# P V of the second and third attention: two column tiles a head, or one full matmul

## What is computed

```python
x = x + jnp.tanh(g_xattn[1]) * attn1(_layernorm(x), ctx)      # plain softmax
x = x + jnp.tanh(g_ffn[1])   * quantised_mlp(_layernorm(x))
x = x + jnp.tanh(g_xattn[2]) * attn2(_layernorm(x), ctx, mask)  # masked softmax
x = x + jnp.tanh(g_ffn[2])   * top2_experts(_layernorm(x))

qh, kh, vh = split_heads(q), split_heads(k), split_heads(v)   # 16 heads of 8
score = einsum('bhqd,bhkd->bhqk', qh, kh) / sqrt(8)
out = einsum('bhqk,bhkd->bhqd', softmax(score), vh)           # this is P V
```

## Time and profile before

| what | value |
| --- | --- |
| median of 3 runs | 2514.34 us (2514.01 to 2516.51) |
| the profiled execution's own time | 2513.01 us |
| its span, first to last instruction | 2511.2 us |
| mean granted TensorE clock | 0.915 |
| second attention, steady step (L1012 to L1012) | 7.44 us |
| third attention, two late steps (1598.4 to 1619.5) | 21.1 us |

### The profile page before, as it was taken

One profiled execution on the slowest core, in us unless ns is written; L12 is line 12 of the kernel. 1 busy time (PEld: TensorE's weight loads), 2 busy tenths in 40 slices (PEclk: granted clock), 3 DMA queues, 4 the chain that ended last, 5 costly groups with the idle time before them and its releaser, 6 DMA issues. The chain is left out here.

```text
span 2511.2 us, 81208 instructions
## 1 busy us (share of the span) xinstructions
PE 2146.8 (85%) x33432; PEld 1717.8 (68%) x33443; DVE 1787.9 (71%) x5105; ACT 1350.6 (54%) x2499; POOL 1157.7 (46%) x1712
## 2 busy tenths in 40 slices
PE   6999999999995969999555799998399958898597
PEld 5887878787874746777444577776399947777375
DVE  3777777777773648887896589886555559988354
ACT  3555555555551327886998455553122259979232
POOL 1333333434343541113776125555466666876444
PEclk8999999999997979998677899997699979989699
DMA  6330000000005621110000111111487622332363
GB/s 194 110 123 27 25 27 25 24 21 20 20 18 152 180 85 55 55 58 17 1 1 3 32 37 52 52 51 36 134 235 230 185 75 79 106 96 79 101 185 103
DMA packets 225233, 195.14 MB, mean 78 GB/s; under 512 B 34444, under 2 KB 197846, under 8 KB 224864
## 3 DMA queue, kind: packets, MB, share of 16 engines
q1 hardware_dynamic: 186336, 143.52, 19.6%
q0 software_dynamic: 18944, 36.98, 4.2%
q10 hardware_dynamic: 19584, 9.44, 1.3%
HBM read 113.53 MB, written 70.55 MB: 73 GB/s over the span
## 5 line engine op out<-in xcount | busy, mean ns | idle before, releaser
L617 POOL DMA_INDIRECT slots<-row,put x256 | 258.1, 1008 | 211.5 <-issue 131.2
L1968 PE MATMUL experts_H<-experts_xs_t,experts_w 128*128 128x256 f32 (+1 forms) x832 | 253.5, 456 | 9.9 <-DMA experts_w<-in_F_w 4.7
L1102 ACT ACTIVATE l_prob_t<-l_banks 128x512 f32<-128x512 f32 x256 | 132.2, 603 | 145.9 <-PE l_banks L1219 115.4
L1968 PEld LDWEIGHTS experts_H<-experts_xs_t,experts_w 128*128 128x128 f32 x832 | 156.7, 195 | 74.5 <-issue 54.0
L1474 POOL TENSOR_TENSOR l_var_eps<-l_mv,eps 128x1 f32<-128x1 f32 x64 | 12.1, 189 | 413.9 <-DVE l_mv L1555 413.9
L1277 PE MATMUL l_banks<-l_val,l_prob_t 128*64 128x18 f32 x5120 | 201.1, 215 | 0.0
L1277 PEld LDWEIGHTS l_banks<-l_val,l_prob_t 128*64 128x64 f32 x5120 | 190.3, 143 | 8.1 <-issue 0.7
L1510 DVE TENSOR_REDUCE l_top<-l_S 128x16 f32<-128x1024 f32 x64 | 78.3, 1224 | 161.7 <-PE l_S L1653 161.7
L1986 PE MATMUL experts_Y<-experts_w,experts_hid 128*128 128x128 f32 x1600 | 190.0, 275 | 3.5 <-DVE experts_y L1912 2.6
L1986 PEld LDWEIGHTS experts_Y<-experts_w,experts_hid 128*128 128x128 f32 x1600 | 184.3, 192 | 5.0 <-issue 4.9
L1823 POOL DMA_INDIRECT rows<-experts_y,experts_idx x144 | 139.9, 971 | 90.0 <-DVE experts_y L1908 52.9
(11 more groups left out here) (312 smaller groups left out, 5943.4 us busy)
## 6 DMA issues: line engine op xcount, KB each, us to landing
experts_w<-in_F_w SPq DMA_DIRECT2D x136, 256.0 KB
l_ctx_t<-in_ctx_t SPq DMA_DIRECT2D x96, 128.0 KB, 2.4
early_q_m<-l_q_t SPq DMA_DIRECT2D x384, 32.0 KB, 1.8
experts_xs<-slots SPq DMA_DIRECT2D x72, 132.0 KB
experts_w<-in_F_w ACTq DMA_DIRECT2D x72, 128.0 KB, 3.3
slots<-l_empty SPq DMA_DIRECT2D x16, 536.0 KB, 4.1
experts_xs<-slots SPq DMA_DIRECT2D x16, 536.0 KB
slots<-l_empty SPq DMA_DIRECT2D x16, 520.0 KB, 5.9
```

The lines of the kernel that those rows point to most:

```text
L617: pool.indirect_dma_start(self.slots, bass.IndirectOffsetOnAxis(ap=g.put[c][:, tile:tile + 1], axis=0), g.row[:, tile, self.sent_cols], No ...
L1102: nc.scalar.activation(prob_t[:, t.par(PROB), r, :], Z[:, r, :], ACT.Exp).then_inc(prob_done, 1)
L1968: last = nc.tensor.matmul(H[:, c, cols], w1_s[:, t.par(2, WS), h, c, :], xs_t[:, t.par(2), cols], start=True, stop=True)
```

## The change

In the second and third attention, one matmul a head takes both tiles: 128 stationary columns (64 queries of each tile) and 36 moving ones (18 of each tile). Of the 128 x 36 result only tile 0's rows with the first 18 columns and tile 1's rows with the last 18 are read. For the 128 columns to lie side by side, the exp writes `prob_t` with the tile inside the head: 128 j + 64 tile + query. The results need 16 x 64 columns and go to Z banks 2 and 3, so P V waits for the exp of bank 3. The reciprocal takes all four sums of a head and partition, 64 a partition instead of 32, and the product is made in two instructions, one for each half of the partitions. The fourth attention ("stable") keeps its form.

```diff
-        recip, ctx_out = ph.sb("recip", [P, 2, 16]), ph.sb("ctx_out", [P, 2, 2, D])
+        recip, ctx_out = ph.sb("recip", [P, 2, 16 if stable else 32]), ph.sb("ctx_out", [P, 2, 2, D])
@@ VectorE, OUT
-                    V.reciprocal(recip[:, :, :], o[:, :, :, 8]).then_inc(recip_done, 1)
+                    pairs = Z[:, 2:4, :].rearrange("p k (h c) -> p (k h) c", c=64)
+                    sums = o[:, :, :, 8] if stable else pairs[:, :, 8:36:9]
+                    V.reciprocal(recip[:, :, :] if stable else recip[:, :, :].rearrange("p k (h s) -> p (k h) s", s=4), sums).then_inc(recip_done, 1)
                     wait(dve, recip_done, t.done(OUT))
-                    V.tensor_tensor(ctx_out[:, t.par(OUT), :, :].rearrange("p b (h c) -> p b h c", c=8), o[:, :, :, 0:8],
+                    if not stable:
+                        for tile in range(2):
+                            rows = slice(64 * tile, 64 * tile + 64)
+                            pair = pairs[rows, :, 18 * tile:18 * tile + 18].rearrange("p h (b c) -> p b h c", c=9)
+                            by = recip[rows, :, :].rearrange("p k (h s) -> p s (k h)", s=4)[:, 2 * tile:2 * tile + 2, :]
+                            last = V.tensor_tensor(ctx_out[rows, t.par(OUT), :, :].rearrange("p b (h c) -> p b h c", c=8),
+                                                   pair[:, :, :, 0:8], by.unsqueeze(3).broadcast_to([64, 2, 16, 8]), ALU.mult)
+                        last.then_inc(o_drained, 1)
@@ ScalarE, PROB
-                            nc.scalar.activation(prob_t[:, t.par(PROB), r, :], Z[:, r, :], ACT.Exp).then_inc(prob_done, 1)
+                            nc.scalar.activation(prob_t[:, t.par(PROB), r, :].rearrange("p (j t n) -> p t j n", t=2, n=64),
+                                                 Z[:, r, :].rearrange("p (t j n) -> p t j n", t=2, n=64), ACT.Exp).then_inc(prob_done, 1)
@@ TensorE, OUT
-                        bank_read(t, 2)
-                    for h in range(16):
-                        terms = [prob_t] if not stable else [soft] if h // 4 < JOINED else [soft, prob_t]
+                        bank_read(t, 3)
+                    for h in range(16 if not stable else 0):
+                        pair = prob_t[:, t.par(OUT), h // 4, P * (h % 4):P * (h % 4) + P]
+                        last = nc.tensor.matmul(Z[:, 2 + h // 8, 64 * (h % 8):64 * (h % 8) + 36], pair,
+                                                val[:, t.par(OUT), :, h, :, :].rearrange("p t b c -> p t (b c)"), start=True, stop=True)
+                    for h in range(16 if stable else 0):
```

More of the change, by code:

```diff
@@ L1038, in step @@
                     wait(dve, o_filled, t.done(OUT))
-                    V.reciprocal(recip[:, :, :], o[:, :, :, 8]).then_inc(recip_done, 1)
+                    pairs = Z[:, 2:4, :].rearrange("p k (h c) -> p (k h) c", c=64)
+                    sums = o[:, :, :, 8] if stable else pairs[:, :, 8:36:9]
+                    V.reciprocal(recip[:, :, :] if stable else recip[:, :, :].rearrange("p k (h s) -> p (k h) s", s=4), sums).then_inc(recip_done, 1)
                     wait(dve, recip_done, t.done(OUT))
-                    V.tensor_tensor(ctx_out[:, t.par(OUT), :, :].rearrange("p b (h c) -> p b h c", c=8), o[:, :, :, 0:8],
+                    if not stable:
[6 more added lines that the diff above has]
+                        last.then_inc(o_drained, 1)
+                    else:
+                        V.tensor_tensor(ctx_out[:, t.par(OUT), :, :].rearrange("p b (h c) -> p b h c", c=8), o[:, :, :, 0:8],
                                     recip[:, :, :].unsqueeze(3).broadcast_to([P, 2, 16, 8]), ALU.mult).then_inc(o_drained, 1)
@@ L1270, in step @@
                     else:
-                        bank_read(t, 2)
-                    for h in range(16):
-                        terms = [prob_t] if not stable else [soft] if h // 4 < JOINED else [soft, prob_t]
+                        bank_read(t, 3)
[4 more added lines that the diff above has]
+                    for h in range(16 if stable else 0):
+                        terms = [soft] if h // 4 < JOINED else [soft, prob_t]
                         for tile in range(2):
```

## The result

The changed kernel takes 2744.82 us (median of 3 runs, 2742.18 to 2754.61) against 2514.34 before: a ratio of 1.0923, 95% interval 1.0881 to 1.0966, so 9.2% slower. The forecast was 2634 with a range of 2598 to 2664. The direction was right, the size was not: the loss of 230 us is nearly twice the 121 us that were forecast.

A forecast was written before the change was run, and what follows sets the result against it. TensorE and VectorE were both nearly full, so their hand-over loop set the step. Added costs of 68 us (second attention), 51 (third) and 2 (later wait) gave 121 us on 2513: 2634 us, 4.8% slower, range 2598 to 2664.

The forecast's parts named there:

- the clock falls: Rival: a tenth of the second and third attention drops to 1.2 GHz, adding 40 us, 2674 us; chance 8%.
- It held 1.00 through 209 us: Argument against a clock fall: TensorE's granted clock stayed 1.00 through the second attention of the kernel before.
- TensorE would idle less than now: Argument against a clock fall: after the change TensorE would have less idle time than in the kernel before.
- +1.62: P V matmuls, us a step: 32 records 110 ns apart take 3.67 us against 2.05.
- record price: Rival: P V pays 29 ns per record whatever its columns, 1.16 us a step; 2508 to 2520 us; chance 5%.
- serial halves: Rival: P V's two half loads already run one after the other, so it keeps 2.05 us; 2538 us; chance 6%.
- Later wait: P V waits for the fourth exp instead of the third: free except in each attention's last steps, 2 us in all.
- Reciprocal: VectorE's reciprocal of 64 elements a partition instead of 32: +0.21 us a step, lower bound +0.03.
- Product: VectorE's product as two instructions of 0.42 us overlapping by 0.08: +0.34 us a step, bounds 0.27 and 0.42.
- The step of 9.56: Second attention: each step grows by 2.12 us from 7.44 to 9.56, 68 us over 32 steps.
- Third attention: Some VectorE extra hidden in its paired steps; pairs go from 21.1 to 24 us, 51 us in all.
- granted clock in the steady steps under 0.95: One of the listed signs in the profile that would prove the forecast wrong.

The follow-up runs named there:

- experiment 3: Kernel before with only VectorE's part of the change (reciprocal of 64 elements, product in two halves), P V unchanged: 2566.9 us, ratio 1.0227.
- experiment 2: Kernel before with each P V matmul of the second and third attention issued twice: 2697.13 us, ratio 1.0736.
- experiment 1: Changed kernel with P V matmuls streaming their 36 columns three times, every eighth head once: 2625.35 us, ratio 1.0464.
- experiment 6: Kernel before with VectorE's part of the change and each P V matmul streaming its 18 columns three times: 2546.87 us, ratio 1.013.

## Why the prediction was wrong

**The step that failed** is the term for the clock. The sum put every step at full clock, and the rival "the clock falls" got 8%, at a price of six or seven steps at 1.2 GHz (40 us). In the run the clock falls behind 44 of 54 P Vs in the two attentions, and its part of the loss is 114 us.

Two arguments stood against it. "It held 1.00 through 209 us" is true of the kernel before and says nothing on the margin: experiment 3 leaves P V alone, adds about 0.6 us a step of VectorE, and loses clock. "TensorE would idle less than now" is wrong twice. In the second attention it idles more, 13.9 of 308 us against 2.3 of 209, since it now waits for the two products (L1314, 13.8 us in all). And it takes busy time in the profile for the activity that holds the clock, which is the real error: experiment 2 idles 1.5 of 280 us and loses the clock, experiment 1 idles 18 of 260 and keeps it. A P V record that loads 128 columns and streams 36 counts as busy through its whole 110 ns. The Trainium skill (TensorE: Matmul & The Clock Gate, The HAM clock gate) says that the clock follows how busy the engine has been recently; the rows here agree only if busy is not read as the profile's busy time. My text had the numbers that should have raised the rival's chance, though no row of before shows how much margin the clock had: half the records, 110 ns each where 58 ns a pair stood, and the same 1152 columns a step in P V (32 x 36 for 64 x 18) spread over 1.6 us more. How much of the fall is owed to the few columns and how much to the longer wait for VectorE no run separates in the changed kernel; 108 columns mend both.

**Where the 229 us are.** First to last L1012 of each attention, the time between them, and the rest, in us of the profiled executions:

| kernel | second | between | third | after | span |
| --- | --- | --- | --- | --- | --- |
| before | 232.0 | 226.9 | 322.7 | 795.7 | 2511.2 |
| experiment 1 (full clock) | 292.0 | 232.3 | 365.8 | 802.7 | 2625.8 |
| the change | 332.7 | 243.4 | 419.1 | 811.5 | 2740.3 |

Ahead of the first L1012 lie 933 to 934 us in all three. From the first row to the second is what P V and VectorE cost: 115 us against the forecast's 121. From the second to the third is what the clock costs: 41 + 11 + 53 + 9 = 114 us, half of the loss.

**P V** (+1.62): right, 3.66 us, its records about 110 ns apart whether they stream 36 or 108 columns. The rivals "record price" and "serial halves" are out.

**Later wait** (2 us in all): the page of the changed kernel has 0.8 us of P V waiting for the exps, less than was counted.

**Reciprocal** (+0.21): 0.56 against 0.36, right. **Product** (+0.34): 0.86 against 0.42, +0.44. The overlap of 0.08 was taken from the L991 pairs, which read SBUF; these two read PSUM and don't overlap (56 of them have a mean of 422 ns, and 0.86 is about twice that). That they differ in where they read is what I see, not a cause that a run has shown. From P V's end to L1062 it is now 9.42 - 7.90 = 1.52 us, against 7.02 - 6.08 = 0.94: +0.58 instead of +0.50, and experiment 6 measures the same 0.6 a step alone.

**The step of 9.56**: the sum is 1.61 + 0.58 = 2.19, and experiment 1 shows 9.53 - 7.44 = 2.09. The missing 0.10 is ahead of P V: L1286 starts 0.44 us after the first L1271, where it was 0.54 before (L1259 to L1277). With no column tiles in P V, no change of tile shape stands between the two; that is the likely reason, not a tested one.

**Third attention**: 24 us a pair forecast, 2 x 12.03 in experiment 1. Its loss from first to last L1012 is 43 us and some of the 7 after; forecast 51. That the kind A steps hide VectorE's extra agrees with this.

**Range and chances**: of what the text listed as proof of error ("granted clock in the steady steps under 0.95"), exactly that came. The upper bound of 2664 held no part of a clock case that lasts. Such a case could be priced: the two groups of score matmuls at 1.93 us instead of 1.04 and 1.12 are 1.7 us more a step, 54 us in the second attention if every step were hit in full. The run shows 41 there, in middle steps of 10.2 to 11.7 us.

## What to carry to other kernels

Before joining tiled matmuls, ask what sets a record: where it is the load, as here, column tiles that load side by side are the gain (58 ns a pair against 110), and four tiles still gain a little over two (0.5% of this kernel) although "issue" holes eat a part of it; a mix of four and two tiles did as well. Then ask how many columns stream in the time: a stretch of load-bound matmuls can be 100% busy in the profile and still cost the clock, and the bill comes in the matmuls behind it, which stream many columns. A cheap test is to stream the same columns twice or three times: where the load hides it, it costs nothing, and if the time falls, the clock was costing time.

## What the runs showed of the hardware

- Behind the same 128-column f32 loads, 18, 36, 72 and 108 streamed columns gave a granted clock of 0.71, 0.81, 0.99 and 1.00 in the second attention, with 3.66 us for a P V at full clock.
- More work can be faster: three times the columns in P V take 4.6% of the time of before off the change, 2.8% off the doubled P V, and 0.3% (0.1 to 0.5) off the kernel before, which is at the edge of what can be told.
- TensorE's clock can be lost by adding VectorE work: 0.94 in the second attention with 0.6 us more a step, back at 1.00 when P V streams more.
- Busy time in the profile doesn't tell whether the clock holds: busy 278.5 of 280 us at 0.86, busy 242 of 260 at 1.00.
- Four column tiles issue f32 records 8.6 ns apart. The Trainium skill (TensorEngine Tiling, Instruction Overhead) gives some 60 cycles to a matmul, by estimate 25 ns at 2.4 GHz; on four tiles side by side the measured spacing is a third of it.
- 128 such records in a row meet holes of 0.3 to 1.6 us in 11 of 28 steps of the second attention. 96 records of the mixed form meet none there, and pauses of 0.2 to 0.4 us in the late steps of the third.
